# A graph network kernel: count-matrix loads issued ahead of stores, a third transpose buffer, and one row one-hot of each group on GpSimd

## The reference

```python
h = maximum(layernorm(x), 0)
for l in range(3):
    mlp = lambda z: maximum(z @ W1[l] + b1[l], 0) @ W2[l] + b2[l]
    agg = segment_sum(mlp(h)[dst], src, num_segments=12500)   # 400000 edges, dst is sorted
    h = mlp(h + agg)
out = x + h @ Wf + bf
```

## Time and profile before

| | |
|---|---|
| median of 3 runs | 2127.72 us (2125.79 to 2129.39) |
| profiled execution | 2123.59 us, span 2121.9 us, mean granted PE clock 0.977 |
| busy over the span | PE 1957.8 us (92%), DVE 1403.5 us (66%), ACT 869.8 us (41%), POOL 551.1 us (26%) |
| chain that ended last | PE 61%, DVE 20%, DMA 7%, issue 5%, ACT 3%, POOL 2%, SP's queue 2% |
| in that chain, by line | PE L1428 57%, DVE L766 10%, DMA arena<-counts_dram 6%, DVE L774 4% |

### The profile page before, as it was taken

How to read it: one execution, slowest core, us unless ns; L and a number is a source line. 1 busy time by engine, 2 the same in 40 slices (tenths; PEclk the granted TensorE clock), 3 DMA queues, 4 the chain that set the end, 5 groups by cost and what they waited for, 6 DMA issues and landing times.

```text
span 2121.9 us, 57789 instructions
## 1 busy us (share of the span) xinstructions
PE 1957.8 (92%) x24911; PEld 1194.8 (56%) x24911; DVE 1403.5 (66%) x1613; ACT 869.8 (41%) x2278; POOL 551.1 (26%) x270
## 2 busy tenths in 40 slices
PE   4656889999999999989999999999999999999998
PEld 3544555555555555555555555555555555555554
DVE  8999999999999999945543343343365433434333
ACT  5986999999989999922200000000010000000000
POOL 2666656666666665500000000000000000000000
PEclk9796999999999999999999999999999999999999
DMA  7356666667666666662544553543544555555452
GB/s 206 92 142 181 184 176 196 197 201 201 196 192 193 198 193 188 190 202 78 161 145 123 168 153 109 182 144 117 170 151 132 168 169 163 161 153 169 140 168 73
DMA packets 332933, 346.21 MB, mean 163 GB/s; under 512 B 21562, under 2 KB 303992, under 8 KB 332184
## 3 DMA queue, kind: packets, MB, share of 16 engines
q1 hardware_dynamic: 327516, 335.59, 54.1%
q0 software_dynamic: 2352, 6.43, 1.2%
q10 hardware_dynamic: 2816, 0.53, 0.2%
HBM read 252.58 MB, written 89.89 MB: 161 GB/s over the span
## 4 chain that ended last, share of the span: by engine, by line
PE 61%; DVE 20%; DMA 7%; issue 5%; ACT 3%; POOL 2%; SPq 2%; DVEq 0%; POOLq 0%; ACTq 0%
PE ps L1428 57%; DVE arena L766 10%; DMA arena<-counts_dram 6%; DVE arena L774 4%; POOL arena L643 2%; SPq L467 2%; DVE arena L808 2%; PE ps L1392 1%; DVE arena L813 1%; PE ps L1540 1%; PE ps L1512 1%; DMA counts_dram<-arena 1%; ACT arena L1198 1%; DVE arena L743 1%; ACT few_far L1183 1%
## 5 line engine op out<-in xcount | busy, mean ns | idle before, releaser
L1428 PE MATMUL ps<-arena,parts 128*64 128x448 fp8e4 x16464 | 1610.9, 354 | 3.8 <-DVE arena L901 1.9
L1428 PEld LDWEIGHTS ps<-arena,parts 128*64 128x64 f16 x16464 | 916.6, 110 | 655.7 <-issue 55.4
L888 DVE TENSOR_SCALAR arena<-arena 128x3136 uint16<-128x3136 uint16 x196 | 191.3, 976 | 574.7 <-PE ps L1428 574.7
L643 POOL TENSOR_TENSOR arena<-arena,weight_now 128x416 int32<-128x416 int32 x196 | 480.3, 2451 | 314.3 <-DVE arena L766 313.6
L1291 ACT ACTIVATE arena<-arena 128x448 f32<-128x448 f32 x42 | 23.9, 577 | 975.0 <-DVE arena L915 975.0
L766 DVE TENSOR_TENSOR arena<-row_iota,key_now 128x3584 f16<-128x3584 f16 (+1 forms) x196 | 403.6, 2059 | 0.0
L1198 ACT ACTIVATE arena<-ps 128x800 uint16<-128x800 f32 x392 | 342.7, 886 | 56.2 <-PE ps L1392 55.2
L1392 PE MATMUL ps<-arena 128*128 128x53 fp8e4 x6272 | 205.7, 190 | 104.9 <-POOL arena L643 88.9
L1392 PEld LDWEIGHTS ps<-arena 128*128 128x128 f16 x6272 | 187.7, 98 | 177.8 <-issue 93.2
L1183 ACT ACTIVATE few_far<-row_iota,few_now 128x128 f16<-128x128 f16 x656 | 214.1, 431 | 0.0
L774 DVE STREAM_TRANSPOSE arena<-arena 128x800 int32<-128x800 int32 x196 | 196.6, 1003 | 5.5 <-DMA counts_dram<-arena 5.5
(11 more groups left out here) (145 smaller groups left out, 841.7 us busy)
## 6 DMA issues: line engine op xcount, KB each, us to landing
arena<-counts_dram SPq DMA_DIRECT2D x294, 784.0 KB, 4.7
counts_dram<-arena SPq DMA_DIRECT2D x784, 100.0 KB, 2.3
h_dram<-parts SPq DMA_DIRECT2D x2, 1536.0 KB, 7.3
edges_dram<-arena SPq DMA_DIRECT2D x2, 1400.0 KB
arena<-in_x_dram SPq DMA_DIRECT2D x14, 192.0 KB
out_dram<-arena SPq DMA_DIRECT2D x14, 192.0 KB
arena<-in_dst_dram SPq DMA_DIRECT2D x1, 1400.0 KB
arena<-in_src_dram SPq DMA_DIRECT2D x1, 1400.0 KB
```

Of the source, the lines that this page charges most:

```text
L643: nc.gpsimd.tensor_tensor(pairs, pairs, weight_now[:, h * HW:(h + 1) * HW].unsqueeze(2).to_broadcast([P, HW, WORDS // 2]), ALU.mult).then_ ...
L888: v.tensor_scalar(spread[:, c % WIDE, 0, :].bitcast(U16), packed, 0x0F0F, None, ALU.bitwise_and)
L1428: last = t.matmul(ps[half(c), b, 0:NB], parts[:, tile, half(part)], spread[:, wide, c ^ exchange, at:at + NB].bitcast(F8), start=start and ...
```

## The change

Four edits are made. (1) In a column whose unit doesn't open a sweep, SP issues both loads before all of the column's stores; a column that opens a sweep keeps the old order. (2) `ctile` has three buffers, with a semaphore each. (3) POOL makes row one-hot 0 of each group (`match_row`, one TENSOR_SCALAR of 128x128 f16 with a pointer scalar); it issues it for group k+1 right behind the weighting of group k, and DVE's row compare covers one row less (31, then 27). (4) Behind the build loop, the first unpack comes between the last two transposes, and it waits for `chunks_multiplied` (the earlier unit's first round) where it waited for `sums_done` (the whole earlier unit).

```diff
+BY_POOL = 1
+TURNED = 3
-        few_now = sb("few_now", [P, HG, FEW], F32)
+        few_now = sb("few_now", [P, HG, BY_POOL + FEW], F32)
-        ctile, build_end = view(at, [2, HBYTES], U8)
+        ctile, build_end = view(at, [TURNED, HBYTES], U8)
-        win, at = view(at, [WR, 2 * WIN], I32)
+        win, at = view(ARENA - WR * 2 * WIN * 4, [WR, 2 * WIN], I32)
...
 # SP: store_counts(k), load_round(n), the column loop
-                                     ctile[q:q + HI, h % 2, :]).then_inc(counts_stored[h % 2], 16)
+                                     ctile[q:q + HI, k % TURNED, :]).then_inc(counts_stored[k % TURNED], 16)
...
                 if c == 0 and u % SB == 0:
-                    for half in counts_stored:
-                        sp.wait_ge(half, 64 * 2 * KG * (u // SB + 1))
+                    groups = HG * KG * (u // SB + 1)
+                    for slot in range(TURNED):
+                        sp.wait_ge(counts_stored[slot], 64 * len(range(slot, groups, TURNED)))
...
+                opens = u >= 0 and u % SB == 0
+                if u >= 0 and not opens:
+                    load_round(ROUND * u)
+                    load_round(ROUND * u + 1)
                 if j:
                     store_counts(j * HG - 2)
                     store_counts(j * HG - 1)
-                if u >= 0:
+                if opens:
                     load_round(ROUND * u)
                 store_counts(j * HG)
-                if u >= 0:
+                if opens:
                     load_round(ROUND * u + 1)
                 store_counts(j * HG + 1)
...
 # POOL
+            def match_row(k):
+
+                pool.wait_ge(s["keys_kept"], k // 2 + 1)
+                if k >= SLOTS:
+                    pool.wait_ge(s["batch_multiplied"], 2 * (k - SLOTS) + 2)
+                nc.gpsimd.tensor_scalar(hot_r[:, k % SLOTS, 0, :], row_iota[:], few_now[:, k % HG, 0:1], 0.0, ALU.add,
+                                        ALU.is_equal).then_inc(s["pool_rows_made"], 1)
...
+            match_row(0)
             for k in range(BUILD * HG):
                 weigh(k)
+                if k + 1 < BUILD * HG:
+                    match_row(k + 1)
                 if k % HG == 2 and k // HG + WR < WT:
                     gather(k // HG + WR)
...
 # DVE: turn_counts(k), make_hots(k), unpack_tail(n), behind the loop
-                if k >= 2:
-                    dve.wait_ge(counts_stored[k % 2], 64 * (k // 2))
+                if k >= TURNED:
+                    dve.wait_ge(counts_stored[k % TURNED], 64 * (k // TURNED))
...
-                few = FEW if k >= FEW_FROM else 0
+                few = BY_POOL + (FEW if k >= FEW_FROM else 0)
...
                 if c == 0 and u > FUSED:
                     dve.wait_ge(s["counts_used"], u - FUSED)
+                elif c == 0:
+                    dve.wait_ge(s["chunks_multiplied"], u)
                 else:
                     dve.wait_ge(s["sums_done"], SBB * u)
...
-            for k in range(BUILD * HG - LAG, BUILD * HG):
-                turn_counts(k)
+            turn_counts(BUILD * HG - 2)
             unpack_tail(ROUND * FUSED)
+            turn_counts(BUILD * HG - 1)
             unpack_tail(ROUND * FUSED + 1)
...
 # ACT: keep_keys copies five keys a group to few_now and waits for pool_rows_made too;
 # the four rows of ACT move to rows 1 to 4.  PE: multiply_group(k)
+                pe.wait_ge(s["pool_rows_made"], k + 1)
```

More of the change, by code:

```diff
@@ L293, in gnn_kernel @@
             "vector_chain", "variance_made", "root_made", "h0_made", "h0_stored", "h0_turned", "h0_kept",
-            "norm_made", "rows_relative", "keys_turned", "keys_kept", "cols_made", "rows_made", "few_far_found", "few_made", "hots_made",
+            "norm_made", "rows_relative", "keys_turned", "keys_kept", "cols_made", "rows_made", "few_far_found", "few_made", "pool_rows_made", "hots_made",
             "batch_multiplied", "batch_kept", "counts_turned",
-                        "counts_stored_0", "counts_stored_1",
+                        "counts_stored_0", "counts_stored_1", "counts_stored_2",
             "hidden0_done", "hidden0_kept", "message0_done", "message_kept",
@@ L311, in gnn_kernel @@
         counts_loaded = [sem(f"counts_loaded_{r}") for r in range(RING)]
-        counts_stored = [s["counts_stored_0"], s["counts_stored_1"]]
+        counts_stored = [s["counts_stored_0"], s["counts_stored_1"], s["counts_stored_2"]]
         chain = [0]
@@ L771, in turn_counts @@
                 dve.wait_ge(s["batch_kept"], 2 * k + 2)
-                if k >= 2:
-                    dve.wait_ge(counts_stored[k % 2], 64 * (k // 2))
-                v.transpose(ctile[:, k % 2, :].bitcast(I32), stage[:, k % 2, :].bitcast(I32)).then_inc(s["counts_turned"], 1)
+                if k >= TURNED:
+                    dve.wait_ge(counts_stored[k % TURNED], 64 * (k // TURNED))
+                v.transpose(ctile[:, k % TURNED, :].bitcast(I32), stage[:, k % 2, :].bitcast(I32)).then_inc(s["counts_turned"], 1)
             def make_hots(k):
@@ L1153, in keep_keys @@
                     act.wait_ge(s["hots_made"], (t - 1) * HG + 2 * u + 2)
+                    act.wait_ge(s["pool_rows_made"], (t - 1) * HG + 2 * u + 2)
                 act.wait_ge(s["keys_turned"], t + 1)
@@ L1157, in keep_keys @@
                 a.activation(few_now[:, 2 * u:2 * u + 2, :], key_bank[:, 0, u * P // 2:(u + 1) * P // 2].rearrange(
-                    "p (h c) -> p h c", h=2)[:, :, 0:FEW], ACT.Copy, scale=-1.0)
+                    "p (h c) -> p h c", h=2)[:, :, 0:BY_POOL + FEW], ACT.Copy, scale=-1.0)
                 a.copy(weight_now[:, u * P // 2:(u + 1) * P // 2], key_bank[:, 2, u * P // 2:(u + 1) * P // 2]).then_inc(
@@ L1182, in find_few_distances @@
                 for c in range(FEW):
-                    last = a.activation(few_far[:, c, :], row_iota[:], ACT.Abs, bias=few_now[:, k % HG, c:c + 1])
+                    last = a.activation(few_far[:, c, :], row_iota[:], ACT.Abs, bias=few_now[:, k % HG, BY_POOL + c:BY_POOL + c + 1])
                 last.then_inc(s["few_far_found"], 1)
@@ L1188, in make_few_rows @@
                 act.wait_ge(s["few_far_found"], k - FEW_FROM + 1)
-                a.activation(hot_r[:, k % SLOTS, 0:FEW, :], few_far[:], ACT.Relu, scale=-RK_UNIT, bias=1.0).then_inc(
+                a.activation(hot_r[:, k % SLOTS, BY_POOL:BY_POOL + FEW, :], few_far[:], ACT.Relu, scale=-RK_UNIT, bias=1.0).then_inc(
                     s["few_made"], 1)
```

## The result

The changed kernel takes 2140.57 us (median of 4 runs, 2139.25 to 2142.55), and the kernel before 2128.19 us in the same series. The ratio is 1.006, with a 95% interval of 1.0043 to 1.0078: **slower by 12.4 us**. I had forecast 2116.6 us and a range up to 2136.

A forecast was written before the change was run, and what follows sets the result against it. DVE was taken to bound the build, busy 731.5 of 750 us. Loads -10.8, row off DVE -12.9, POOL's row +17.6 and loop end -5.0 sum to -11.1 us: 2127.7 to 2116.6 us, range 2102 to 2136.

The forecast's parts named there:

- Nothing else moves with it: In the build, POOL's new row operation was to delay no weighting or gather; at h = 2 both end before the row compare.
- a weighting made late: In the build, a named way to be wrong: the new operation delays POOL's weighting, seen as more PE waits for L643.
- loads earlier: In the build, loads issued before the column's stores remove DVE's waits for loads except at sweep openings: 10.8 us gained.
- end of the loop, third buffer: Behind the build loop, PE's 5.15 us wait for the first unpack nearly goes: 5.0 us gained.
- the row taken from DVE, 196 groups: In the build, DVE's row compare loses one row, 66 ns a group over 196 groups: 12.9 us gained.
- direct price of POOL's row: In the build, POOL's new operation holds DVE for 0.09 us in each of 196 groups: 17.6 us lost.
- my two bounds, 0.04 and 0.22: DVE time lost per build group to POOL's row, in us: 7.8 us in all at 0.04, 43 at 0.22.
- the break-even of 0.146: Price of POOL's row in us per build group at which the whole change gains nothing, 28.7 / 196.
- part 2: In the build, one row of DVE's compare moves to POOL: 12.9 us gained, 17.6 lost, +4.7 us by itself.
- The rival that ended slower, at 2142: In the build, POOL's row comes first each time and holds DVE 0.22 us a group: +14.4 us; chance 0.22.
- The rival in which the waits for loads come back as waits for PE: In the build at L808, PE falls behind and the 10.8 us are not gained: 2127.4 us, no change; chance 0.13.

## Why the prediction was wrong

**The step that failed** is the paragraph "Nothing else moves with it". It said of h = 2 that "the new operation and the gather end before that compare does". I had moved the gather by the new operation's time and kept its duration of 1.3 us. But that duration holds only when the gather is issued before the row compare, as in all columns of the kernel before. Issued behind its start, the gather ends 0.84 to 0.93 us after the compare does, 2.5 to 2.7 us on record, and the weighting follows behind the transpose's room, where DVE's unpack pays for it. The experiment without a row and with a late gather shows this by itself, at 23.7 us; moving the gather to h = 0 gives 21.5 us back. The reasoning I had used for the weighting in the earlier trace rows applied to the gather too, and I didn't apply it. I had also named a weighting made late as a way to be wrong. I looked for its price in PE's waits, though, and it was paid in DVE's unpack.

The other terms, with what they measured:

| term | forecast | measured |
|---|---|---|
| loads earlier | -10.8 | -17.5 alone |
| end of the loop, third buffer | -5.0 | -3.8 alone |
| both | -15.8 | -20.3 |
| the row taken from DVE, 196 groups | -12.9 | -12.0 (403.1 to 391.1 us busy) |
| direct price of POOL's row | +17.6 (0.09) | +24.0 (0.122) |
| late gather and weighting | 0 | +21.5 |
| sum | -11.1 | +13.2 (12.4 by the medians) |

The direct price follows from 2119.07 - 2107.03 = 12.0 us, plus the 12.0 that the shorter compares save, over 196 groups. It is a price in time: what VectorE's operations grew by is 27 us, and some of that hides in waits. The measured terms are differences between successive kernels, so that they add up is no proof of them. The 24.0 us between the forecast 2116.6 and 2140.57 are, to within 0.3, 21.5 of late gather, 6.4 of direct price and 0.9 of smaller saving, less 4.5 that the loads and the end gave beyond the forecast. The direct price lies between my two bounds, 0.04 and 0.22, and below the break-even of 0.146 that I gave. So part 2 was a loss by itself, as forecast, but of 12.0 and not 4.7 us. Without the late gather the change would have come out at 2119, and that this is only 2.5 us above my forecast is in part luck: the dearer row and the larger gain from the loads nearly cancel. The rival that ended slower, at 2142, had a chance of 0.22, and its mechanism, POOL coming first each time, is what the timeline shows: L660 starts 0.10 to 0.11 us ahead of DVE's operation in the groups shown of the changed kernel and of the one with the gather at h = 0. But it pays 0.15 us and not 0.22. It takes the late gather as well to bring the kernel to 2140.6, so the closeness of that rival's time is chance.

The rival in which the waits for loads come back as waits for PE is out: 0.7 us of them are left.

The Trainium skill's rule in "SBUF — State Buffer", section "Who interferes with whom", agrees with DVE's 1.85 us: the unpack loses about as much as the whole weighting takes, 0.91 us. It fits the row's price less well: by it the later one to issue should be held for the whole instruction, and DVE loses 0.15 us to an operation that takes 0.59 us beside the transpose. On the gather the same section infers that a compare of two tensors should not hold up descriptor writing, and here a gather issued during one takes 2.5 to 2.7 us against 1.3 to 1.4. The measurement decides. It doesn't show which of the gather's steps waits: reading its 128 offsets from SBUF would explain it too, and no run tests that.

**What is best.** The change without POOL's row: 2107.03 us, 0.9908 of before.

## What to carry to other kernels

Where two engines exclude each other, look for the room that the slower one really has (here one transpose a group, 0.93 us, with 0.75 used by the weighting) and price a new operation by what no longer fits, not by its own duration. Then go through everything queued behind it and ask of each whether it still starts before the next long exclusive operation: here a gather that missed that start by 0.14 us ended 1.3 us later than one on time. Durations read from a trace hold only for the order in which they were taken.

## What the hardware showed that I had not expected

- An indirect gather on GpSimd's queue takes 1.4 us if issued ahead of VectorE's 2 us compare of two SBUF tensors and 2.5 to 2.7 us if issued 0.14 to 0.35 us behind its start. In both cases it ends 0.84 to 0.93 us behind the end of the compare that was under way when it was issued, be it the column or the row compare. Issued during an unpack (the gather at h = 0), it ends 0.91 us behind the unpack's end, 606.24 and 605.33.
- A GpSimd TENSOR_SCALAR of 128x128 f16 with a pointer scalar holds VectorE's operation for only 0.15 us if issued 0.1 us ahead of it, though it stays on record for 1.33 us, until behind that operation's end, and the operation after that is longer by 0.09 us too (1.05 from 0.96, with two unpacks in a row). Put in front of the weighting, in the transpose's room, the same operation takes 0.59 us. Why it holds VectorE for less time than it runs wasn't settled; a read and a write that are granted apart would fit, and no run tests it.
